# A GRU recurrence with W_hh as the moving operand: four column tiles, one transpose, one tanh for r and z

## The reference

```python
def cell(h, x):
    gi = x @ W_ih + b_ih                 # W_ih: 512 x 1536
    gh = h @ W_hh + b_hh                 # W_hh: 512 x 1536
    i_r, i_z, i_n = jnp.split(gi, 3, axis=-1)
    h_r, h_z, h_n = jnp.split(gh, 3, axis=-1)
    r = jax.nn.sigmoid(i_r + h_r)
    z = jax.nn.sigmoid(i_z + h_z)
    n = jnp.tanh(i_n + r * h_n)
    h_new = (1.0 - z) * n + z * h
    return (h_new, h_new)
```

## Time and profile before

| | |
|---|---|
| Median of 3 runs | 1959.59 us |
| The three runs | 1957.7, 1959.59, 1968.15 us |
| Span of the profiled execution, first to last instruction | 1957.8 us |
| Mean granted TensorE clock | 0.929 |
| TensorE matmuls busy | 1641.2 us, 84%, 32972 of them |
| TensorE weight loads busy | 1251.9 us, 64% |
| VectorE busy | 1636.9 us, 84%, 5843 instructions |
| ScalarE busy | 635.5 us, 32% |
| GpSimd busy | 643.7 us, 33% |
| Mean rate of all DMAs | 41 GB/s |

### The profile page before, as it was taken

How to read it: one execution, slowest core, us unless ns; L and a number is a source line. 1 busy time by engine, 2 the same in 40 slices (tenths; PEclk the granted TensorE clock), 3 DMA queues, 4 the chain that set the end, 5 groups by cost and what they waited for, 6 DMA issues and landing times. The chain is left out here.

```text
span 1957.8 us, 82261 instructions
## 1 busy us (share of the span) xinstructions
PE 1641.2 (84%) x32972; PEld 1251.9 (64%) x32972; DVE 1636.9 (84%) x5843; ACT 635.5 (32%) x1711; POOL 643.7 (33%) x795
## 2 busy tenths in 40 slices
PE   5422347999999999999999999999999999999976
PEld 2211115776777777777777777777777777777764
DVE  8999887888888888888888888888888888887653
ACT  1111223433333333333333333333333333333331
POOL 4545323333333333333333332333333333332111
PEclk8755568999999999999999999999999999999997
DMA  7313120000000000000000000000000000000100
GB/s 264 135 59 124 40 97 23 25 30 31 22 19 27 30 30 30 30 30 30 30 30 29 26 30 30 30 30 30 30 30 30 27 17 24 30 25 27 33 14 18
DMA packets 35405, 80.45 MB, mean 41 GB/s; under 512 B 4864, under 2 KB 5248, under 8 KB 34688
## 3 DMA queue, kind: packets, MB, share of 16 engines
q1 hardware_dynamic: 28080, 63.09, 9.6%
q10 hardware_dynamic: 6992, 12.13, 1.8%
HBM read 58.43 MB, written 16.78 MB: 38 GB/s over the span
## 5 line engine op out<-in xcount | busy, mean ns | idle before, releaser
L1294 PE MATMUL ps_rn<-hx,whh 128*128 128x32 f16 x16384 | 451.2, 176 | 85.0 <-DVE hx L715 47.4
L1294 PEld LDWEIGHTS ps_rn<-hx,whh 128*128 128x128 f16 x16384 | 430.9, 96 | 129.8 <-DVE hx L715 90.3
L1016 POOL COPY hT_steps<-hx 128x128 f16<-128x128 f16 x256 | 120.2, 469 | 992.3 <-DVE hx L715 992.3
L1187 PE MATMUL ps_gi<-x1T,wih 128*128 128x128 f16 x4608 | 289.6, 219 | 1.2 <-ACT gi L523 1.2
L1187 PEld LDWEIGHTS ps_gi<-x1T,wih 128*128 128x128 f16 x4608 | 271.3, 98 | 25.9 <-issue 1.7
L532 ACT ACTIVATE r<-r_pre,scale 128x64 f32<-128x64 f32 x256 | 89.0, 348 | 581.6 <-DVE r_pre L735 581.6
L1294 PE MATMUL ps_z<-hx,whh 128*128 128x32 f16 x8192 | 244.2, 176 | 0.0
L1294 PEld LDWEIGHTS ps_z<-hx,whh 128*128 128x128 f16 x8192 | 223.5, 96 | 0.1
L523 ACT ACTIVATE gi<-ps_gi,b_i,scale_x 128x128 f32 (+1 forms) x384 | 144.4, 456 | 159.1 <-PE ps_gi L1187 159.1
L1003 POOL TENSOR_TENSOR qf<-f8c,fe 128x512 bf16<-128x512 bf16 x128 | 135.8, 1061 | 148.4 <-DVE f8c L796 148.4
L1120 PE MATMUL ps_gate_up<-wq,qxT 128*128 128x512 bf16 x512 | 143.6, 397 | 19.5 <-issue 15.0
(11 more groups left out here) (198 smaller groups left out, 2885.2 us busy)
## 6 DMA issues: line engine op xcount, KB each, us to landing
wih<-in_x_steps ACTq DMA_DIRECT2D x32, 256.0 KB, 5.5
xin<-in_x_steps SPq DMA_DIRECT2D x32, 256.0 KB, 4.0
xres<-in_x_steps SPq DMA_DIRECT2D x32, 256.0 KB, 4.1
x_dram<-x SPq DMA_DIRECT2D x32, 256.0 KB, 2.9
x_in<-x_dram SPq DMA_DIRECT2D x32, 256.0 KB, 2.7
out_rows<-y SPq DMA_DIRECT2D x32, 256.0 KB, 2.0
wst<-in_ffn_w SPq DMA_DIRECT2D x12, 512.0 KB, 3.4
sg_gs<-in_ffn_w SPq DMA_DIRECT2D x12, 512.0 KB, 3.7
```

Source lines behind the costliest of these rows:

```text
L1016: g.tensor_copy(hT_steps[:, :, s, :], hx[:, :, :, :].rearrange("p k u b -> p (k u) b"))\
L1187: last = mm(ps_gi[:, j * P:(j + 1) * P], wih_parts[:, k, at:at + P], x1T[:, x, k, :], start=k + w + x == 0, stop=k == KD - 1 and w == 1)
L1294: last = mm(ps[:, (at + j) * 2 * B:(at + j + 1) * 2 * B], whh[:, k, u, gate * D + j * P:gate * D + (j + 1) * P], hx[:, k, :, :].rearrange( ...
```

## The change

- **Operands swapped.** The state is now the stationary operand, 128 rows x 32 columns (high and low part of 16 sequences), and W_hh moves past it. Each of four groups of 32 array columns gets the same state and its own quarter of the columns of W_hh, the c-th 32 of every 128, for all three gates: 12 pieces of 32 make 384 columns. There are 4 chunks k, 2 parts w and 4 groups: 32 matmuls of 384 columns, accumulated in one bank `ps_rzn`, where group g writes partitions 32g to 32g+31.
- **One transpose.** The result has sequences on partitions. One VectorE transpose of 32 x 32 blocks turns 128 x 384 from PSUM into `turned` in SBUF, which has the old layout for all gates.
- **Joint sums.** `gi` holds its parts in the order n, r, z, bias, so that one add of 192 elements brings gi for r and z and the bias for n (`half`), and a second adds the low part (`pre`).
- **Tanh for sigmoid.** sigmoid(x) = (1 + tanh(x/2))/2. One tanh makes r and z from 128 elements; the factors of two go into the following instructions. The update is written as z h and (z - 1) n, of which `less_z` and `zh` don't need n.
- **Silu.** ScalarE makes the silu of the gate product and of the router's hidden layer; the products L823 and L839 go.
- **Shares.** One difference, one tanh, and two GpSimd instructions that make the two shares, ahead of `c0`.
- Buffers of the weight part are laid over others (`wst`, `wm`), with one more wait on SyncE before the first `xres` load.

```diff
-            def state_products(ps, at, gate):
-                for j in range(KD):
-                    for k in range(KD):
-                        for u in range(2):
-                            last = mm(ps[:, (at + j) * 2 * B:(at + j + 1) * 2 * B],
-                                      whh[:, k, u, gate * D + j * P:gate * D + (j + 1) * P],
-                                      hx[:, k, :, :].rearrange("p u b -> p (u b)"), start=k + u == 0,
-                                      stop=k + u == KD)
+            def state_products():
+                for w in range(2):
+                    for k in range(KD):
+                        moving = whh[:, k, w, :].rearrange("p (q g c) -> p q g c", q=3 * KD, g=GROUPS)
+                        for g in range(GROUPS):
+                            last = mm(ps_rzn[g * 32:(g + 1) * 32, 0:3 * P],
+                                      hx[:, k, :, :].rearrange("p u b -> p (u b)"), moving[:, :, g, :],
+                                      start=k + w == 0, stop=k + w == KD)
                 return last
...
                     pe.wait_ge(hx_ok, c * STEPS + (s + 1))
-                    state_products(ps_rn, 0, GATE_R)
-                    state_products(ps_rn, KD, GATE_N).then_inc(rn_mm, 1)
-                    state_products(ps_z, 0, GATE_Z).then_inc(z_mm, 1)
+                    state_products().then_inc(rzn_mm, 1)
...
-                dve.wait_ge(rn_mm, t1)
-                v.tensor_tensor(by_chunk(r_half[:, :]), r_both[:, :, 0, :], gi_step(c, GATE_R, s),
-                                ALU.add).then_inc(r_half_ok, 1)
...
+                dve.wait_ge(rzn_mm, t1)
+                v.transpose(turned[:, :, :, :, :], ps_rzn[:, 0:6 * HB]).then_inc(turn_ok, 1)
+                dve.wait_ge(turn_ok, t1)
+                both = turned[:, :, :, :, :].rearrange("p q k u b -> p (q k) u b")
+                v.tensor_tensor(half[:, :, :, :], both[:, :, 0, :], gi_rz_and_bias(c, s), ALU.add).then_inc(half_ok, 1)
+                dve.wait_ge(half_ok, t1)
+                v.tensor_tensor(pre[:, :, :, :], both[:, :, 1, :], half[:, :, :, :], ALU.add).then_inc(pre_ok, 1)
                 beside(1)
...
+                dve.wait_ge(rz_ok, t1)
+                v.scalar_tensor_tensor(by_chunk(rn[:, :]), by_chunk(r_tanh), 1.0, pre[:, 2, :, :], ALU.add,
+                                       ALU.mult).then_inc(rn_ok, 1)
                 dve.wait_ge(rn_ok, t1)
+                v.scalar_tensor_tensor(by_chunk(n_pre[:, :]), gi_step(c, GATE_N, s), 2.0, by_chunk(rn[:, :]), ALU.mult,
+                                       ALU.add).then_inc(n_pre_ok, 1)
                 beside(2)
                 wait(dve, hcopy, c * STEPS + s)
+                v.tensor_scalar(less_z[:, :], z_tanh, 1.0, HALF_S_H, ALU.subtract, ALU.mult)
+                v.scalar_tensor_tensor(zh[:, :], z_tanh, 1.0, h[:, :], ALU.add, ALU.mult).then_inc(zh_ok, 1)
+                dve.wait_ge(zh_ok, t1)
                 dve.wait_ge(n_ok, t1)
...
+                v.tensor_tensor(zn[:, :], less_z[:, :], n[:, :], ALU.mult).then_inc(zn_ok, 1)
+                dve.wait_ge(zn_ok, t1)
+                v.scalar_tensor_tensor(hx[:, :, 0, :], by_chunk(zh[:, :]), 0.5, by_chunk(zn[:, :]), ALU.mult,
+                                       ALU.subtract).then_inc(hx_hi, 1)
...
-                    act.wait_ge(r_pre_ok, t1)
-                    nc.scalar.activation(r[:, :], r_pre[:, :], ACT.Sigmoid, scale=S_INV).then_inc(r_ok, 1)
+                    act.wait_ge(pre_ok, t1)
+                    nc.scalar.activation(rz_tanh[:, :], pre[:, 0:2, :, :], ACT.Tanh, scale=HALF_S_INV).then_inc(rz_ok, 1)
                     act.wait_ge(n_pre_ok, t1)
-                    nc.scalar.activation(n[:, :], n_pre[:, :], ACT.Tanh, scale=S_INV).then_inc(n_ok, 1)
-                    act.wait_ge(z_pre_ok, t1)
-                    nc.scalar.activation(z[:, :], z_pre[:, :], ACT.Sigmoid, scale=S_INV).then_inc(z_ok, 1)
+                    nc.scalar.activation(n[:, :], n_pre[:, :], ACT.Tanh, scale=HALF_S_INV).then_inc(n_ok, 1)
...
                     act.wait_ge(gate_mm, count(f, NF, s // 2 + 1))
-                    wait(act, gs_done, count(f, NF, s // 2))
-                    nc.scalar.activation(sg[:, :], ps_gate[:, :], ACT.Sigmoid).then_inc(sg_done, 1)
+                    wait(act, inter_done, count(f, NF, s // 2))
+                    nc.scalar.activation(gs, ps_gate[:, :], ACT.Silu).then_inc(gs_done, 1)
...
-                    if F:
-                        dve.wait_ge(sg_done, count(f, NF, s // 2 + 1))
-                        v.tensor_tensor(gs[:, :], ps_gate[:, :], sg[:, :], ALU.mult).then_inc(gs_done, 1)
...
+                    pool.wait_ge(gap_ok, count(l, 1, 1))
+                    wait_apart(pool, passed)
+                    for place, sign in enumerate((0.5, -0.5)):
+                        g.tensor_scalar(share[:, place:place + 1], gap_tanh[:, :], sign, 0.5, ALU.mult,
+                                        ALU.add).then_inc(share_ok, 1)
                     for place, c_one in enumerate((c0, c1)):
-                        pool.wait_ge(share_ok, count(l, 1, 1))
+                        pool.wait_ge(share_ok, count(l, 2, 2))
```

More of the change, by code:

```diff
@@ L159, in build @@
         x_row = sb("x_row", [1, 2])
[L161 removed]
+        gi = sb("gi", [P, 2 * GI_PARTS * D])
         h = sb("h", [P, HB])
         hx = sb("hx", [P, KD, 2, B], F16)
[L164 to L166 removed]
+        turned = sb("state_products_turned", [P, 3, KD, 2, B])
+        half, pre = sb("half_sums", [P, 3, KD, B]), sb("pre_activations", [P, 3, KD, B])
+        rz_tanh, rn, n_pre, n = (sb("rz_tanh", [P, 2 * HB]), sb("rn", [P, HB]), sb("n_pre", [P, HB]), sb("n", [P, HB]))
+        r_tanh, z_tanh = rz_tanh[:, 0:HB], rz_tanh[:, HB:2 * HB]
+        less_z, zh, zn = (sb(x, [P, HB]) for x in ("less_z", "zh", "zn"))
         hT_steps, hT_tile = sb("hT_steps", [P, 2 * KD, STEPS, B], F16), sb("hT_tile", [P, 2 * KD, P], F16)
[L169 removed]
+        in_bias = sb("x1_in_bias", [P, 2 * D])
+        x1_in, x1_bias, y = in_bias[:, 0:D], in_bias[:, D:2 * D], sb("y", [P, D])
         xa = sb("xa", [P, ROUTE])
[L171 removed]
+        hid_pre, hid = sb("hid_pre", [P, HID]), sb("hid", [P, HID])
         hidT = sb("hidT", [HID, P])
@@ L505, in others @@
                     wait(act, x_ev, count(e, 1))
+                    wait(act, gi_ev, count(e, 3))
                     nc.scalar.activation(scale_x[:, :], ps_x_scale, ACT.Copy).then_inc(x_scale_ok, 1)
@@ L836, in others @@
                                            ALU.add).then_inc(hp_ok, 1)
-                if L and here == (2, 0):
-                    dve.wait_ge(hs_ok, count(l, 1, 1))
-                    v.tensor_tensor(hid[:, :], hid_pre[:, :], hid_sg[:, :], ALU.mult).then_inc(hid_ok, 1)
                 if L and here == (4, 0):
```

126 lines of the change are left out of this document (57 added, 69 removed).

## The result

| | before | changed |
|---|---|---|
| median of the runs | 1960.26 us (4 runs) | 2038.72 us (4 runs, 2037.5 to 2040.6) |
| profiled execution: span | 1957.8 us | 2035.6 us |
| first product of the recurrence | 335.1 us | 324.8 us |
| first product of the last step | 1931.4 us | 2007.9 us |

The ratio is 1.0398, 95% interval 1.0375 to 1.0421: 4% slower. The preparation became 10 us shorter; the recurrence, from its first product to that of its last step, went from 1596 to 1683 us, 87 longer.

What follows compares the result with a forecast made beforehand. The step-to-step chain through VectorE was taken as the bound, not busy TensorE. +2.25 us a tile over 27 full tiles (+61) and +10 for 40 light steps gave 2030 us, 3.6% slower; range 1930 to 2125.

Steps and rivals of the forecast that it cites:

- Products: TensorE's 32 matmuls per step: four column tiles side by side, 1.29 us, results landing after 1.6, 0.3 earlier than before.
- Vector chain: Transpose, two joint sums, tanh and update to hx's low part: 3.73 us a step against 3.18, 0.55 longer.
- Silu: Silu on ScalarE removes VectorE's L823 product in the four odd steps, counted as 0.60 us each; hid's as 0.13.
- Steps 1, 2 and 5: Steps of a full tile: -0.05 us in 1 and 5 (silu against chain), -0.45 in 2 (a VectorE wait goes).
- Step 3: Full tile: half and pre, reading SBUF, wait for GpSimd's xg and qf; +1.05 us.
- Step 4: Full tile: VectorE has no slack and saves nothing, so the longer chain costs +0.55 us.
- This widens the range only: TensorE at 1.2 GHz: products 2.6 us, +1.3 a step, up to 20 us at the end; not in the sum.
- Step 6: Full tile: GpSimd's two share instructions delay coeff and wxa by 0.45 us, the chain adds 0.55; +1.0 us.
- Steps 7 and 0: Stretch set by TensorE's list: 1.41 us of issue time stays, chain +0.55, earlier landing -0.3; +0.2 us.
- Light steps: The 40 steps outside the 27 full tiles, near the bare chain: +0.55 - 0.3 = +0.25 us each, +10 us.
- no wait for GpSimd: Rival: half, pre and the share instructions find cover in steps 3 and 6, tile even; 1970 us, chance 0.12.
- TensorE's relief: Rival: TensorE's work, 7.6 us less a tile, shows through if the vector chain hardly lengthens; 1890 us, chance 0.2.

Runs made afterwards that it cites:

- experiment 7: Changed kernel with two tiles to one loop turn, so gi's buffer address is known beforehand in every step; 2019.46 us.
- the last kernel: Changed kernel with the old recurrence put back, shares on ScalarE, and one more tile ahead of the loop on VectorE alone; 1939.78 us.
- experiment 3: Changed kernel with eight idle products of 512 columns added on TensorE in step 3, results unread; 2029.41 us.
- experiment 5: Changed kernel with GpSimd's two full-width layer norm operations of step 2 (gamma, beta) cut to 8 columns; 1973.88 us.
- experiment 2: Changed kernel with only the products put back: 96 with W_hh stationary into one bank, joint sums kept, no transpose; 2052.93 us.
- experiments 1 and 12: 1: changed kernel with the old recurrence put back, 1986.73 us; 12: the same plus shares on ScalarE and one more tile ahead of VectorE's loop, 1939.78 us.
- experiment 4: Changed kernel with the two routing shares made on ScalarE instead of GpSimd; 2017.64 us.

## Why the prediction was right, and where its sum was not

The forecast was 2030 us, the median 2038.72, inside the range. The mechanism held: the chain through VectorE, and GpSimd in steps 3 and 6. By its own steps, forecast and measured:

- *Products*: 1.29 us of issue, landing after 1.6; measured 1.48 in all, landing after 1.53. The 34 us which the ratio for row tiles of the Trainium skill, "TensorE: Matmul & The Clock Gate", Part 3, would have added are not there.
- *Vector chain*: 3.73, measured 3.75 outside the loop. Inside it is 3.95, against 3.28 before: 0.67 longer where the sum has 0.55. The sum did not have the address from the loop's register (experiment 7: 0.2 us a step, of which the kernel before pays 0.1).
- *Silu*: 0.60 a step; the row of 0.681 lay over a wait of f8c for f, which now shows. Before, it was 1.63 us from f's start to f8c's end, now 1.26: 0.37. And of the steps 3, 5 and 7 it pays in 5 alone. In the last kernel, which has it with the old recurrence, step 5 is 0.36 shorter, steps 3 and 7 as before.
- *Steps 1, 2 and 5*: -0.05, -0.45, -0.05; measured -0.25, -0.30, +0.31. Step 5 is those two terms: 0.67 for the chain less 0.37 for the silu.
- *Step 3*: +1.05; measured +1.30, by the rows that the forecast named, though I had f8c out of it: it is held by xg for 1.1 us.
- *Step 4*: +0.55; measured +1.24 by the medians, +1.13 by the means. The step that failed is "This widens the range only", of the clock: after step 3 TensorE idles 2.67 us and in 17 of 27 full tiles comes back at the lower clock (experiment 3 gets 0.43 us a tile back), and the loop's address adds its 0.1. A clock at half level inside the full tiles was one of the signs of being wrong, and it was there.
- *Step 6*: +1.0; measured +1.35, of it 0.54 for the shares (0.45 forecast).
- *Steps 7 and 0*: +0.2; measured -0.90 (+0.72 and -1.62). "1.41 us of issue time before 1048.93 stay" failed: that time was the loading of 768 products' program, and it went with the products.
- *A tile*: +2.25 forecast, +2.75 by the medians of the table; the 27 full tiles together +69 (forecast +61). *Light steps*: +0.25 forecast, +0.45 measured, 18 us for the 40 (forecast 10). Eight of them, the last tile, make 8 of the 18: five of its steps have their products at the lower clock. *The preparation*: "less than 2 us", measured -10. The three tiles ahead of the recurrence hold 12 of L823's products, 8 us on VectorE, which is busy 108 of 135 us there; that this is the cause was not tried.

69 + 18 - 10 = 77, of 77.8 between the profiled spans and 78.5 between the medians. Errors of the sum cancelled: steps 1 to 6 came out 1.6 us a tile dearer than forecast and steps 7 and 0 1.1 cheaper, and the preparation's 10 us, which were not foreseen, stand against the full tiles' and the light steps' 16. That the total came within 9 us of the forecast is in part luck, and says less than the steps do.

Of the rivals, "no wait for GpSimd" is the one that experiment 5 makes real, with two operations left out: the tile is then 51.7 us and the time 1974, near its 1970. "TensorE's relief" fell as it was put, by faster products: TensorE's busy time dropped to 38.5 us in 51, and every wait of its products was for hx. What did show through was the shorter program, in step 0.

What stays open: why VectorE's loop is loaded anew at one place in its program and not at another, beyond that it hangs on the place (147 packets against 30 and 29, with the same body); why the clock falls in some tiles and not in others after the same wait; and how the 78 us divide in a full tile. In a light step the chain can be divided by the starts of its rows (kernel before, experiment 2, changed kernel): the transpose adds 0.61 us, the joint sums with the longer tanh 0.32, the new update takes 0.36 off, 0.57 in all.

## What to carry to other kernels

In a recurrence, what the matrix engine saves counts only as far as the next reader is waiting. Two wide sums that depend on each other put rn 1.29 us behind the first of them (light steps of experiment 2), where the narrow ones, with independent ones in their gaps, put it at 0.97; 0.05 of the difference is ScalarE's longer tanh. And a wide operation that moves its inputs from PSUM to SBUF gets a new rival, GpSimd. Before believing a small difference between two kernels with a long loop, compare the packets of each engine's instruction queue: here 49 us of TensorE's waits and, in one experiment, 72 of VectorE's hung on them, and moving VectorE's loop by one tile was worth an estimated 26 us (the 47 between experiments 1 and 12, less the 21 that the shares gave in experiment 4).
